# Edge columns of the image patches as 12 more rows of the eight pixel offsets, moved there by transfers

## Reference

```python
xs = jnp.concatenate([x] + [_shift(x, s) for s in shifts], axis=1)
t = xs.reshape(B, C5, h, PATCH, w, PATCH).transpose(0, 2, 4, 3, 5, 1).reshape(B, h * w, PATCH * PATCH * C5)
tn = (t - mu) * jax.lax.rsqrt(var + EPS) * ln_gamma + ln_beta
return jnp.einsum('bnp,pd->bnd', tn, W) + b
```

## Time and profile before

| | us |
|---|---|
| median of 3 runs (1895.81 to 1897.97) | 1896.07 |
| the profiled execution | 1889.4 |
| its span, first to last instruction | 1887.7 |
| TensorE busy | 1579.8 (84%) |
| VectorE busy | 1364.8 (72%) |
| ScalarE busy | 1283.7 (68%) |
| GpSimd busy | 1089.7 (58%) |
| DMA queue of SP | 131.00 MB, 44.4% of 16 engines |

### The profile page before, as it was taken

How to read it: one execution, slowest core, us unless ns; L and a number is a source line. 1 busy time by engine, 2 the same in 40 slices (tenths; PEclk the granted TensorE clock), 3 DMA queues, 4 the chain that set the end, 5 groups by cost and what they waited for, 6 DMA issues and landing times.

```text
span 1887.7 us, 50796 instructions
## 1 busy us (share of the span) xinstructions
PE 1579.8 (84%) x16574; PEld 1297.6 (69%) x16574; DVE 1364.8 (72%) x3151; ACT 1283.7 (68%) x1958; POOL 1089.7 (58%) x1503
## 2 busy tenths in 40 slices
PE   0539999999999999999999999999466666666666
PEld 0427788888888888888888888887345555555555
DVE  3636676767767676767676767676389999999996
ACT  1226666766767676767676666665288888888887
POOL 5035555555555555555555555554177777777775
PEclk9869999999999999999999999999666666666665
DMA  8674666665657565756565666660000000000000
GB/s 102 141 127 59 95 87 96 86 99 83 103 79 104 83 99 83 99 88 94 89 94 91 91 93 88 94 87 25 17 16 21 21 21 22 22 22 22 22 22 26
DMA packets 159967, 132.96 MB, mean 70 GB/s; under 512 B 32558, under 2 KB 151040, under 8 KB 159808
## 3 DMA queue, kind: packets, MB, share of 16 engines
q1 hardware_dynamic: 159168, 131.00, 44.4%
q0 software_dynamic: 768, 1.57, 0.5%
HBM read 118.32 MB, written 11.91 MB: 69 GB/s over the span
## 4 chain that ended last, share of the span: by engine, by line
PE 66%; DVE 15%; issue 7%; SPq 3%; ACT 3%; DMA 3%; POOL 1%; DVEq 1%; ACTq 0%; POOLq 0%
PE ps L1092 20%; PE ps L1176 8%; PE ps L1259 7%; PE ps L1250 7%; PE ps L1206 4%; DVE ff_st L860 4%; PE ps L1238 3%; PE ps L1232 3%; PE ps L1211 3%; PE ps L1336 2%; PE ps L1355 2%; DVE xpix L841 2%; PE ps L1167 2%; DVE xpix L853 1%; PE ps L1157 1%
## 5 line engine op out<-in xcount | busy, mean ns | idle before, releaser
L1092 PE MATMUL ps<-w_eff,pix 118*112 118x193 f32 (+1 forms) x2048 | 408.4, 337 | 25.0 <-ACT pix L909 24.3
L927 ACT ACTIVATE probs<-ps,isw 116x688 f32<-116x688 f32 x384 | 299.2, 831 | 171.6 <-PE ps L1238 171.6
L527 POOL TENSOR_TENSOR xpix<-probs,g_b 112x192 f32<-112x192 f32 (+1 forms) x512 | 296.5, 609 | 109.1 <-ACT probs L1044 99.7
L741 DVE TENSOR_REDUCE nmax<-ps 116x12 bf16<-116x1344 f32 (+2 forms) x192 | 299.6, 1560 | 80.2 <-PE ps L1211 77.7
L452 POOL TENSOR_TENSOR xsq<-xsq 118x784 f32<-118x784 f32 (+2 forms) x192 | 221.8, 1155 | 218.5 <-ACT xsq L920 208.4
L1092 PEld LDWEIGHTS ps<-w_eff,pix 118*112 118x112 f32 (+1 forms) x2048 | 309.8, 167 | 52.4 <-issue 18.9
L472 POOL TENSOR_SCALAR_AFFINE_SELECT probs<-probs 116x464 f32<-116x464 f32 x384 | 268.2, 717 | 46.5 <-ACT probs L927 31.0
L909 ACT ACTIVATE pix<-xpix 118x896 f32<-118x896 f32 (+1 forms) x128 | 198.4, 1552 | 104.9 <-DMA xpix<-in_x 56.0
L457 POOL TENSOR_TENSOR front_st<-front_st,expo 128x2 f32<-128x2 f32 x64 | 45.0, 703 | 235.2 <-DVE front_st L693 221.2
L1336 PE MATMUL ps<-w1t,xpix 96*112 96x384 f16 (+1 forms) x512 | 160.7, 488 | 14.6 <-ACT xpix L1035 13.3
L685 DVE TENSOR_SCALAR front_st<-ps 112x1 f32<-112x1 f32 (+1 forms) x128 | 18.3, 151 | 213.8 <-PE ps L1157 202.4
(11 more groups left out here) (161 smaller groups left out, 3363.3 us busy)
## 6 DMA issues: line engine op xcount, KB each, us to landing
xpix<-in_x SPq DMA_DIRECT2D x192, 196.0 KB
xpix<-in_x SPq DMA_DIRECT2D x192, 195.1 KB
rden<-den_rows SPq DMA_DIRECT2D x256, 85.5 KB, 2.1
out<-xpix SPq DMA_DIRECT2D x64, 87.0 KB
out<-xpix SPq DMA_DIRECT2D x64, 84.0 KB
xpix<-in_x SPq DMA_DIRECT2D x128, 34.1 KB
xpix<-in_x SPq DMA_DIRECT2D x128, 34.0 KB
den<-o_sb SPq DMA_DIRECT2D x256, 2.7 KB
```

What stands on the lines that cost most here:

```text
L527: last = nc.gpsimd.tensor_tensor(v2[0:P, b, tile, cols], gel[0:P, b, tile, cols], g2_b[0:P, cols], ALU.mult)
L741: V.tensor_reduce(dst, src, AX_X, ALU.max, negate=True).then_inc(s_mx, 1)
L927: A(probs[0:TB, g, 2 * e:2 * e + 2, :], ps[0:TB, 4 + 2 * e:6 + 2 * e, 0:SK], ACT.Exp, scale=isw[0:TB, 7:8]).then_inc(s_p, 1)
L1092: last = MM(ps_tok[tile][0:P, :], src, w_eff[0:HI, o, :], start=(o == 0), stop=(o == OFFS - 1))
```

## The change

The ninth offset is gone. `OFFS` is 8, and each offset has 120 rows in place of 118: rows 0 to 53 and 54 to 107 are the two copies of the image (the second one moves from partition 64 to 54), and the 96 border rows (48 left, 48 right) are spread as 6 + 6 rows over the eight offsets, since 6 rows x 8 offsets hold 48. GpSimd fills one buffer `side` with one copy, SP moves it with two transfers into rows 108 to 119 of `pix` (`place_sides`), and the same is done once with the weights in `w_eff` (three transfers). `patches` does 2 x 8 products, the fourth part ends at 13 of 16, `add_squares` has three additions, `edge_squares` two squares in place of three, and the setup of the weights one copy on VectorE in place of four. GpSimd copies an image's side pixels one step earlier, at the end of its step. `place_sides(m)` waits for that copy and for the last patch product of image m-1, which still reads the rows. In SP's step it stands between `turn_denominators(n)` and the load.

```diff
-OFFS = PATCH // 2 + 1
-LO, HI = CH * (PATCH + 2), 64 + CH * (PATCH + 2)
+OFFS = PATCH // 2
+LO = CH * (PATCH + 2)
+EDGE = CH * PATCH // OFFS
+HI = 2 * (LO + EDGE)
...
-        side = [sb(f"side{i}", [128, IMG_TOK]) for i in range(2)]
+        side = sb("side", [128, IMG_TOK])
...
-                for first, col in ((0, 0), (64, 1)):
+                for first, col in ((0, 0), (LO, 1)):
...
+            def place_sides(m):
+
+                if isinstance(m, int) and m == 0:
+                    sp.wait_ge(s_side0, 1)
+                else:
+                    sp.wait_ge(s_side, m)
+                    sp.wait_ge(s_front, m)
+                for half, shift in ((0, 1), (1, 0)):
+                    row, first = 2 * LO + EDGE * half, LO * half
+                    sp.dma_start(pix[row:row + EDGE, :, shift:IMG_TOK],
+                                 side[first:first + CH * PATCH, 0:IMG_TOK - shift]).then_inc(s_place, 16)
+
             sp.wait_ge(s_pad, 3)
             load_pixels(0, 0)
+            sp.wait_ge(s_weff, 1)
+            sp.dma_start(w_eff[LO:2 * LO, :, 0:DIM],
+                         wacc[0:LO, 2:18, :].rearrange("p (m e) d -> p m e d", e=2)[:, :, 0, :]).then_inc(s_wmove, 16)
+            for half, col in ((0, 0), (1, PATCH + 1)):
+                row = 2 * LO + EDGE * half
+                sp.dma_start(w_eff[row:row + EDGE, :, 0:DIM], wacc[0:CH * PATCH, col, :]).then_inc(s_wmove, 16)
+            place_sides(0)
...
             def next_pixels(m, par):
                 sp.wait_ge(s_pix, 2 * (m + 1))
-                sp.wait_ge(s_side, 2 * (m + 1))
                 load_pixels(m + 2, par)
...
             next_pixels(0, 0)
+            place_sides(1)
             next_pixels(1, 1)
+            place_sides(2)
             next_pixels(2, 0)
-
-            def step_images(n, par, old=True, load=True):
+            place_sides(3)
+
+            def step_images(n, par, old=True, load=True, place=True):
                 if old:
                     turn_denominators(n)
+                if place:
+                    place_sides(n + 4)
                 if load:
                     next_pixels(n + 3, par)
...
             def sides(m, par, count):
 
                 pool.wait_ge(s_x[par], 16 * XDMA * count)
-                edge = [t.rearrange("p (h w) -> p h w", h=GRID) for t in (side[par][:, :], xpix[par][:, :])]
-                src = edge[1][:, :, PATCH - 1:SIDE - 1:PATCH]
-                after(pool, s_lrstd, m - 1)
+                after(pool, s_place, 32 * m)
+                edge, src = [t[0:2 * LO].rearrange("p (h w) -> p h w", h=GRID) for t in (side, xpix[par])]
                 apart(pool)
-                nc.gpsimd.tensor_copy(edge[0][0:LO, :, 1:GRID], src[0:LO]).then_inc(s_side, 1)
-                pool.wait_ge(s_side, 2 * m + 1)
-                apart(pool)
-                nc.gpsimd.tensor_copy(edge[0][64:HI, :, 0:GRID - 1], src[64:HI]).then_inc(s_side, 1)
-                pool.wait_ge(s_side, 2 * m + 2)
+                nc.gpsimd.tensor_copy(edge[:, :, 0:GRID - 1], src[:, :, PATCH - 1:SIDE - 1:PATCH]).then_inc(
+                    s_side0 if isinstance(m, int) and m == 0 else s_side, 1)
...
-                                                  (xsq[0:HI, 0, :], xsq[0:HI, 0, :], xsq[0:HI, 1, :]),
-                                                  (ssq_sb[0:HI, :], xsq[0:HI, 0, :], xsq[0:HI, 8, :]))):
+                                                  (ssq_sb[0:HI, :], xsq[0:HI, 0, :], xsq[0:HI, 1, :]))):
...
-                if newest:
-                    sides(n + 3, par, count)
...
                 if newest:
                     add_squares(n + 3)
-
-            step_images(-2, 1, 1, old=False)
...
+                if coming is not None:
+                    sides(n + 4, par, coming)
...
-            step(V.tensor_copy(w_eff[0:LO, 0:8, 0:DIM], inner[:, :, 0, :]))
-            step(V.tensor_copy(w_eff[64:HI, 0:8, 0:DIM], inner[:, :, 1, :]))
-            step(V.tensor_copy(w_eff[0:LO, 8, 0:DIM], wacc[0:LO, 0, :]))
-            step(V.tensor_copy(w_eff[64:HI, 8, 0:DIM], wacc[0:LO, 17, :]))
+            dve.sem_inc(s_weff, 1)
+            step(V.tensor_copy(w_eff[0:LO, :, 0:DIM], inner[:, :, 0, :]))
...
-            def edge_squares(m, par):
+            def edge_squares(m):
                 act.wait_ge(s_pix, 2 * (m + 1))
-                after(act, s_ssq, 4 * m)
-                act.wait_ge(s_side, 2 * (m + 1))
-                for o in (0, 7):
+                act.wait_ge(s_place, 32 * (m + 1))
+                after(act, s_ssq, ADDS * m)
+                for o in (0, OFFS - 1):
                     A(xsq[0:HI, o, :], pix[0:HI, o, :], ACT.Square, scale=mult_root[0:HI, o:o + 1])
-                A(xsq[0:HI, 8, :], side[par][0:HI, :], ACT.Square, scale=mult_root[0:HI, 8:9])
...
                 if first == 0:
                     pe.wait_ge(s_pix, 2 * (m + 1))
-                    pe.wait_ge(s_side, 2 * (m + 1))
+                    pe.wait_ge(s_place, 32 * (m + 1))
                     after(pe, s_tokrd, m)
...
-                    if o < 8:
-                        src = pix[0:HI, o, lo:lo + P]
-                    else:
-                        src = side[par][0:HI, lo:lo + P]
+                    src = pix[0:HI, o, lo:lo + P]
...
-            P1, P2, P3, P4 = 2, 4, 9, 14
+            P1, P2, P3, P4 = 2, 4, 9, 13
```

More of the change, by code:

```diff
@@ L39 @@
 EPS_LN, EPS_RMS = 1e-5, 1e-6
-READY1, READY2 = 36, 52
+READY1, READY2 = 33, 49
 N_W = HIDDEN * DIM
@@ L90, in build @@
         bias_q = sb("bias_q", [128, DIM])
-        pix = sb("pix", [128, 8, IMG_TOK])
+        pix = sb("pix", [128, OFFS, IMG_TOK])
         fold = sb("fold", [128, PER * HD], F16)
@@ L253, in build @@
         XDMA = 10
+        ADDS = 3
         MXR = 3
@@ L406, in _ @@
             for n in range(IMAGES - 5, IMAGES):
-                step_images(n, None, load=False)
+                step_images(n, None, load=False, place=n + 4 < IMAGES)
             with sp.Fori(0, IMAGES) as n:
@@ L423, in _ @@
                 nc.gpsimd.memset(clear, 0.0).then_inc(s_zero, 1)
-            for clear in (xpix[0][:, :], side[0][:, :], side[1][:, :]):
+            for clear in (xpix[0][:, :], side[:, :], pix[:, :, :]):
                 nc.gpsimd.memset(clear, 0.0).then_inc(s_pad, 1)
@@ L481, in _, with step_images @@
             add_squares(0)
-            def step_images(n, par, count, old=True, newer=True, newest=True):
+            sides(1, 1, 1)
+            def step_images(n, par, coming, old=True, newer=True, newest=True):
                 if newer:
@@ L497, in step_images @@
                     add_squares(n + 3)
-            step_images(-2, 1, 1, old=False)
-            step_images(-1, 0, 2, old=False)
-            step_images(0, 1, 2)
-            step_images(1, 0, 3)
+                if coming is not None:
+                    sides(n + 4, par, coming)
+            step_images(-2, 0, 2, old=False)
+            step_images(-1, 1, 2, old=False)
+            step_images(0, 0, 3)
+            step_images(1, 1, 3)
             with pool.Fori(1, PAIRS - 2) as t:
                 for par in range(2):
[L505 to L508, removed]
+                    step_images(2 * t + par, par, t + 3)
+            step_images(IMAGES - 4, 0, None)
+            step_images(IMAGES - 3, 1, None, newest=False)
+            step_images(IMAGES - 2, 0, None, newer=False, newest=False)
             step_images(IMAGES - 1, 0, None, newer=False, newest=False)
@@ L1077, in _, with patches @@
             MM, TR = nc.tensor.matmul, nc.tensor.transpose
-            def patches(m, par, first, end):
+            def patches(m, first, end):
                 if first == 0:
                     pe.wait_ge(s_pix, 2 * (m + 1))
-                    pe.wait_ge(s_side, 2 * (m + 1))
+                    pe.wait_ge(s_place, 32 * (m + 1))
                     after(pe, s_tokrd, m)
@@ L1118, in _ @@
             last.then_inc(s_tset, 1)
-            pe.wait_ge(s_weff, 1)
-            patches(0, 0, 0, 2 * OFFS)
+            pe.wait_ge(s_weff, 2)
+            pe.wait_ge(s_wmove, 48)
+            patches(0, 0, 2 * OFFS)
             pe.wait_ge(s_vset, READY2)
@@ L1269, in part_of_patches @@
                     if newest:
-                        patches(n + 3, par, first, end)
+                        patches(n + 3, first, end)
                 if old:
@@ L1401, in shape_constants @@
     mult = np.zeros((128, OFFS), np.float32)
-    mult[0:LO, 0:8] = count[:, 1:17:2]
-    mult[64:HI, 0:8] = count[:, 2:17:2]
-    mult[0:LO, 8], mult[64:HI, 8] = count[:, 0], count[:, 17]
-    assert (mult[:, 1:7] == mult[:, 1:2]).all()
+    mult[0:LO], mult[LO:2 * LO] = count[:, 1:17:2], count[:, 2:18:2]
+    for half, col in ((0, 0), (1, PATCH + 1)):
+        row = 2 * LO + EDGE * half
+        mult[row:row + EDGE] = count[0:CH * PATCH, col].reshape(EDGE, OFFS)
+    assert (mult[:, 1:OFFS - 1] == mult[:, 1:2]).all()
     cf[:, 256:256 + MULT] = np.concatenate([mult, np.sqrt(mult)], axis=1)
```

20 lines of the change are left out of this document (12 added, 8 removed).

## The result

The changed kernel takes 1991.35 us (median of 4 runs, 1987.51 to 2003.23) where the kernel before took 1897.02 on the same chip: ratio 1.0505, 95% interval 1.0458 to 1.0551. The forecast was 1982. The profiled execution took 1990.6 us, of which the span is 1988.8, against 1887.7 before: 101.1 us more.

The account below looks back on a forecast made before the run. Two loops bind: TensorE's 18.68 us step and the load loop through SP, 18.5 us, growing to 20.1. Loop 80 + prologue 8 - setup 1 - end 0.7 = +86 us, median 1982 us, range 1918 to 2045.

Parts of the forecast that it names:

- Two loops of one length: TensorE's 18.68 us step and the load loop through SP, 18.5 us, bind together; shortening one gives at most 0.2 us.
- The placing's price: SP between broadcast and load: two waits and two transfer issues add 2 x 0.76 + 0.1 = 1.6 us a step.
- The bounds 0.6 and 2.4: Limits in us on SP's two placing issues, from an edge transfer of the load and the text rows' transfer.
- The step: Image loop: the loop through SP becomes 20.1 us, so each step grows 1.38 us, 58 steps by 80 us.
- The clock in the gaps: Rival: TensorE's clock halves after its new gaps, +0.65 us a step if in all 58, 2020 us; chance 0.12.
- C: Rival theory in the experiments: TensorE's clock falling in the gaps is most of the loss.
- Before the loop: Prologue: patches(1) waits for placed rows behind load 2, until 134.45, +8 us; setup about 1 us less.
- The end: After load 63, one step still has patch products and gains 0.69 us.
- The sum: Whole kernel: 80 + 8 - 1 - 0.7 = +86 us.
- The faster rival: TensorE sets the step, so the two products are gained in full, 42 us: 1854 us; chance 0.05.
- Issues for nothing: Rival: the two placing issues cost SP almost nothing, only the prologue's +6 us remains, about 1901 us; chance 0.05.
- A longer load: Rival: placing runs on the load's last engines lengthen each load up to 1.4 us, 81 us more, 2063; chance 0.06.

Follow-up runs that it names:

- The products alone: The kernel before without the ninth offset's products, its border columns missing from the result: 1876.46 against 1890.04 us, 0.9936.
- the issues alone: The kernel before plus two transfers a step of the placing's shape into a buffer nobody reads: 1992.54 against 1890.04 us, 1.053.

## Why the prediction was right, point by point

- **Two loops of one length.** Right. The products alone gave 13.6 us of 42, the issues alone cost +5.3%.
- **The placing's price.** 1.6 us predicted, 1.77 measured in the changed kernel and 2.42 - 0.78 = 1.64 for the bare issues: 755 ns each (median of 128), near `den<-o_sb` with 690, the row that it was taken from. The bounds 0.6 and 2.4 were far off on both sides. The section "Anatomy of one DMA — SWDGE (gpsimd) path" of the Trainium skill's "DMA: Bandwidth & Descriptors", which I set against it, describes transfers issued from GpSimd and gives descriptor generation no figure, so its 50 ns was no price for SyncE's issue, and the 0.1 us that I drew from it was a wrong reading.
- **The step.** 20.1 predicted, 20.07 measured, but so close only by luck, since three errors cancel. The load became 0.47 us shorter (13.47, not 13.94), where the forecast kept it. The placing cost 0.17 more. And the step is 20.07 - 19.81 = 0.26 us over its loop, which is the next point.
- **The clock in the gaps.** Given 0.12 as a case of its own, it came in two fifths of that size. TensorE in windows of 4 us (busy, granted clock, DMA share, GB/s), after its wait of 2.05 us at 803.44 and after one of 2.13 us at 846.43:

```profile
800.00:804.00 4.00, 1.95 (x14) 1.00 0.04 8
804.00:808.00 4.00, 4.00 (x33) 0.58 0.35 101
808.00:812.00 4.00, 4.00 (x21) 0.50 0.99 139
...
844.00:848.00 4.00, 1.86 (x23) 1.00 0.08 15
848.00:852.00 4.00, 4.00 (x58) 1.00 0.41 116
```

  The first gap is followed by 0.50, which is 1.2 GHz: the products of the queries then take nearly twice as long:

```profile
806.46 4.91 PE L1197 MATMUL ps<-xnT,wq_pad 97*128 97x228 f32 x12
...
828.38 2.57 PE L1197 MATMUL ps<-xnT,wq_pad 97*128 97x228 f32 x12
```

  The denominators of that step are on time (`invert` waits 0.58), and TensorE, not the loop, makes it 22.9 us long from load to load. The second gap is followed by the full clock. Between 200 and 1280 us the clock is at half for 75 us in the changed kernel, 31 in the one with the bare issues, 0 before. What sorts the gaps stays open. Its price can be read from the steps: in six of the 58 the clock is at half for 7 or 10 us, the denominators are on time, and the six take 134.1 us together, 15.2 more than six loops of 19.81. These are the whole 0.26 us a step and 15 us of the 101, where the rival had 38. So C is real and small.
- **Before the loop.** +7 predicted, +13.4 measured up to load 5, of which 1.8 is that load's own placing. patches(1), expected near 134, stands at 138.19:

```profile
138.19 1.60 PE L1112 MATMUL ps<-w_eff,pix 120*112 120x193 f32 x4 [28.72 <-DMA pix<-side]
```

  The placed rows behind load 2 are what it waits for, as forecast; the size was off. SP issues them at 125.64, and they land 12.6 us later. Of the setup I expected 1 us less and got 2.3 more: the text rows' transfers, which open SP's way to load 1, start at 102.81 and not at 100.48. I put it down to a term that the forecast left at nothing, the first placing: patches(0) waits 10.29 us for its placed rows and starts at 83.94, where it started at 79.58.
- **The end.** 0.7 us less expected, 9.8 more measured. From the denominators of image 63 to the end it is 548.7 against 542.2 us, in code that the change doesn't touch, and the same stretch measures 540.7 to 550.6 over the twelve experiments, so I attribute none of these 6.5 us. The other 3.3 lie between load 63 and those denominators (90.3 against 87.0); the bare issues have 89.6 too, the products alone 87.2. I put them down to the loop's last late step, which I had left out; no run shows it apart.
- **The sum.** +86 predicted, +101 in the profiles, +94 in the medians. In the profiles the 58 steps came 2 us under the forecast (77.9 for 80), the stretch ahead of them 6 us over it and the stretch behind them 10.5 us over it.
- **The faster rival.** Refuted by the products alone. **Issues for nothing:** refuted, 0.755 us each. **A longer load:** not in the changed kernel, where the placing goes 1.6 us ahead; where it goes with the load, the load is 0.77 us longer.

No version tried beats the kernel before with the whole result; the placing on ScalarE comes within 0.3% of it.

## What to carry to other kernels

Before you take work from the busiest engine, write down every loop of waits that comes back once a step, the one through the queue that issues transfers too, and add up its length: two products a step less were worth 0.2 us, two transfers a step more cost 1.8. A transfer has two prices, the issuer's time by its shape and the engines that it spreads over; splitting raised the first and merging spoiled the second, both by more than was to be gained. Where work is moved by transfers, put them on the queue whose stretch between two waits has room, and look at what they then travel beside.

## What the runs showed of the hardware that I had not expected

- SP's time for one transfer goes by its shape, not its bytes: 0.25 us for 3 partitions of 13 runs, 0.75 for one partition of 13 runs, 0.41 for a broadcast of 2.7 KB to 32 partitions, 0.59 for the same to 128, 0.755 from 48 partitions to 6 x 8, and 0.768 for this last shape with runs of 60 values in place of 195 or 196. ScalarE takes 0.741 for the placing, GpSimd 0.619 for the first.
- The same load to partitions 0 to 107 is some 0.5 us shorter than to 0 to 53 and 64 to 117 (13.34 and 13.47 against 13.88, 13.94 and 14.07), where the placing goes out ahead of it; with the placing behind it the load takes 13.70, with the placing beside it 14.24. Why was not tried.
- The denominators, issued behind a load on one queue, land 0.70 to 0.72 us (means) after the load's last row in every kernel where they were late, however much earlier than that they were issued; the placed rows, issued behind a load, land 0.43 us after it.
- TensorE's wait of 2.05 us before 803.44 was followed by some 10 us at half clock, the wait of 2.13 us before 846.43 by none.
